# Four narrow q·k rows as one f32 product each on TensorE, where they were two f16 halves

## The chip, the cores and the metric

The kernel runs on one core of a Trainium2 chip. A NeuronCore has a matrix engine (TensorE, in the profile PE, its weight loads apart as PEld), three engines for elementwise work (VectorE or DVE, ScalarE or ACT, GpSimd or POOL) and a queue for DMAs (SyncE or SP). They run side by side and wait for each other through semaphores; each takes its own instructions strictly in the order in which they are written. The metric is the device time of one execution in microseconds, the median of several.

## The reference, cut to what matters

One layer of a model with x of 4 x 1024 x 256: half a gated feed-forward part, an attention part with a delta rule, and again half a feed-forward part, each behind a LayerNorm.

```python
x = x + 0.5 * ffn(layernorm(x))
x = x + attn(layernorm(x))
x = x + 0.5 * ffn(layernorm(x))

# ffn: ternary weights with a scale for each output
h = silu(lin(x, w1)) * lin(x, w2)
h = gelu(lin(h, h1)); h = gelu(lin(h, h2)); return lin(h, w3)

# attn: 16 heads of 16, one step for each of the 1024 tokens
retrieval = einsum('bhij,bhj->bhi', S, k_t)
S = S + einsum('bhi,bhj->bhij', beta_t * (v_t - retrieval), k_t)
o_t = einsum('bhij,bhj->bhi', S, q_t)
```

## The kernel before

**Tiling.** The tokens are cut into 8 slabs of 128 tokens for each of the 4 sequences. The feed-forward layers run over a slab at a time (512 columns; at the two ends over half a slab, 256 columns), with fp8 weights and the activations split into two f16 halves, high and low, so every product is two matmuls: L1066 for the first layer, L1083 for the others. The attention runs over 16 parts, each a half slab, in chunks of 16 tokens. What the step of the reference does one token at a time is done by chunks: the products of all pairs of tokens inside a chunk (k·k and q·k) are formed first, then a triangular solve, and the state S is brought in once a chunk.

**The rows.** A row t of k·k or q·k holds the products of token t of every chunk with the tokens before it (for q·k with itself too). Row t of q·k has 32 times (t + 1) columns, so the rows qk 0 to qk 3 have 32, 64, 96 and 128 columns, and row 15 has 512. The 128 partitions are 8 heads of 16; the sum over the 16 elements of a head is a matmul with a constant matrix of ones and zeros (`head_ones`, for k·k `head_minus`). A row goes through these steps:

- GpSimd multiplies k or q by k, elementwise, into a buffer of `pairs` (L594), f32.
- A row that is in `SPLIT` is then cut into halves: ScalarE casts it to f16 (`pairs_hi`, L728), GpSimd subtracts and casts the rest (`pairs_lo`, L602), and TensorE multiplies `head_ones16` with the one and the other into the same bank (L1118, L1119).
- A row that is not in `SPLIT` goes to TensorE as it is, one f32 matmul (L1121). The profile shows an f32 matmul as two records of TensorE and two weight loads.
- VectorE takes the sum from the bank (L885 and L887 for q·k, L867 to L871 for k·k).

Before the change `SPLIT` holds the k·k rows 6 to 15 and all 16 rows of q·k. The k·k rows 1 to 5 (32 to 160 columns) go as f32. There are 16 parts, so each row occurs 16 times; only k·k row 0 does not exist.

**What sets the order.** The order on every engine is written out ahead of time. The feed-forward work is a stream of slots; a frame of attention is 88 ticks laid over this stream, and at each tick the attention's work is put between the slots. In the frame of a part, its q·k rows stand at the ticks `E_QK` of the frame behind (1, 4, 6, 7 for rows 0 to 3, then 12, 14, 16 ...), its k·k rows at `E_KK` of the frame ahead (54 to 87, the f32 rows last). A planner gives the ticks of the steps ahead of the matmul: the product of a split row is made 9 ticks ahead (`PAIR_LEAD["half"]`), its high half is cast 4 and its low half 3 ticks ahead; the product of a whole row is made 4 ticks ahead (`PAIR_LEAD["whole"]`). The times move later where a buffer is not free by the plan: there are 6 buffers of `pairs` and 5 of each half. A buffer of `pairs` is free after the low half is made if its row was split, and after the matmul if it was whole:

```python
if before in SPLIT:
    pool.wait_ge(pairs_ready, q - PAIR_BUFFERS + 1)
else:
    pool.wait_ge(att_filled, U[before] + 1)
```

GpSimd makes in the same queue the low halves of the feed-forward activations (`hid_lo`, L565), for which TensorE waits too, and ScalarE the functions and the high halves in front of them (L680, L656).

Of the kernel before, what the change touches and what calls it, by code (L numbers as in the profile page):

```python
# [178 lines left out]
    READ.update({use: 1 + i for i, use in enumerate(u for u in USES if READER[u[0]] == _reader)})  # L179
DOTS = [use for use in USES if use[0] in ("kk", "qk")]  # L180
DOT = {use: q for q, use in enumerate(DOTS)}
SPLIT_FROM = {"kk": 6, "qk": 0}
SPLIT = {use: q for q, use in enumerate(u for u in DOTS if u[2] >= SPLIT_FROM[u[0]])}
SPLITS = list(SPLIT)

# [1032 lines left out]
```

## Time and profile before

| | us |
|---|---|
| median of 3 runs | 1817.11 |
| lowest, highest | 1815.38, 1817.98 |
| the profiled execution | 1814.47 |
| its span, first to last instruction | 1812.8 |
| TensorE busy in it | 1729.3 |
| VectorE, ScalarE, GpSimd busy | 1242.2, 1055.7, 1208.6 |

The rows of the trace stand in numbered groups further down. A busy time of TensorE counts a matmul up to its modelled end, so that matmuls overlap in it; what a matmul costs the engine is read from the start of the one behind it. "Idle before" is the time in which an engine stood still ahead of an instruction, with what ended it.

### The profile page before, as it was taken

The numbers are of one execution on the slowest core, as the hardware profiler recorded it, in microseconds if no ns is written. First come the engines' busy times: TensorE is split into PE (matmuls) and PEld (weight loads), VectorE is DVE, ScalarE is ACT, GpSimd is POOL, SyncE is SP. The second block draws the span as 40 slices with busy tenths as digits, with TensorE's granted clock in tenths as the row PEclk, the third lists the DMA queues.
The fourth block names the chain that finished last, engine by engine and source line by source line (L and its number), as shares of the span: only waits on it lengthen the run. The fifth ranks groups of instructions, "written<-read, shape, count | busy, mean of one in ns | idle before, by whom it ended". The sixth has DMA issues, their size and how long they took to land.

```text
span 1812.8 us, 29738 instructions
## 1 busy us (share of the span) xinstructions
PE 1729.3 (95%) x10030; PEld 1068.9 (59%) x10030; DVE 1242.2 (69%) x2890; ACT 1055.7 (58%) x2115; POOL 1208.6 (67%) x1501
## 2 busy tenths in 40 slices
PE   6989989999999999999999999999999999999999
PEld 5855555555555555555555555578655555555588
DVE  5255776777776877868767687777776768777331
ACT  4656555474656565656556474656656555655454
POOL 4463876767676767777676667667776767675653
PEclk9999999999999999999999999999999999999999
DMA  7100000000000000000000000000000000000000
GB/s 289 44 1 1 1 1 1 1 1 2 0 1 1 24 1 24 1 1 1 1 2 1 1 24 1 1 25 1 1 1 1 1 1 13 1 1 12 1 13 13
DMA packets 5270, 23.16 MB, mean 13 GB/s; under 512 B 640, under 2 KB 1664, under 8 KB 3584
## 3 DMA queue, kind: packets, MB, share of 16 engines
q1 hardware_dynamic: 5120, 21.26, 3.2%
q8 instruction: 82, 1.34, 0.3%
q14 instruction: 68, 0.56, 0.1%
HBM read 17.06 MB, written 4.19 MB: 12 GB/s over the span
## 4 chain that ended last, share of the span: by engine, by line
PE 65%; DVE 10%; issue 8%; POOL 8%; ACT 7%; POOLq 0%; ACTq 0%; DVEq 0%
PE ffn_bank L1083 40%; PE ffn_bank L1066 5%; PE att_bank L1131 5%; PE att_bank L1103 4%; POOL hid_lo L565 3%; PE state_bank L1139 2%; PE att_bank L1118 2%; POOL pairs_lo L602 2%; PE ln_bank L1024 2%; PE att_bank L1119 2%; POOL pairs L594 2%; ACT hid L680 2%; DVE hid L821 1%; ACT L680 1%; DVE terms L920 1%
## 5 line engine op out<-in xcount | busy, mean ns | idle before, releaser
L1083 PE MATMUL ffn_bank<-hid_hi,w_sb 128*128 128x512 f16 (+1 forms) x2736 | 905.9, 346 | 7.8 <-ACT gate L667 4.6
L1083 PE MATMUL ffn_bank<-hid_lo,w_sb 128*128 128x512 f16 (+1 forms) x2736 | 905.8, 346 | 0.0
L565 POOL TENSOR_TENSOR hid_lo<-hid,hid_hi 128x512 f16<-128x512 f32 (+1 forms) x456 | 462.7, 1030 | 296.2 <-ACT hid_hi L656 295.9
L594 POOL TENSOR_TENSOR pairs<-KQ 128x32 f32<-128x32 f32 (+15 forms) x496 | 325.7, 667 | 123.8 <-DVE KQ L848 104.8
L1083 PEld LDWEIGHTS ffn_bank<-hid_hi,w_sb 128*128 128x128 fp8e4 x2736 | 275.9, 101 | 206.5 <-issue 11.3
L1083 PEld LDWEIGHTS ffn_bank<-hid_lo,w_sb 128*128 128x128 fp8e4 x2736 | 268.6, 98 | 205.7 <-issue 12.4
L602 POOL TENSOR_TENSOR pairs_lo<-pairs,pairs_hi 128x448 f16<-128x448 f32 (+15 forms) x416 | 313.0, 757 | 74.0 <-ACT pairs_hi L728 73.7
L728 ACT CAST pairs_hi<-pairs 128x448 f16<-128x448 f32 (+15 forms) x416 | 174.8, 438 | 158.9 <-POOL pairs L594 157.6
L656 ACT CAST hid_hi<-hid 128x512 f16<-128x512 f32 (+1 forms) x456 | 234.9, 552 | 30.7 <-DVE hid L821 30.0
L680 ACT ACTIVATE hid<-ffn_bank,par_sb 128x512 f32<-128x512 f32 (+1 forms) x304 | 171.7, 616 | 123.5 <-PE ffn_bank L1083 122.8
L1066 PE MATMUL ffn_bank<-xn_hi,w_sb 128*128 128x512 f16 (+1 forms) x532 | 177.6, 348 | 9.1 <-DVE hid L821 6.6
L1066 PE MATMUL ffn_bank<-xn_lo,w_sb 128*128 128x512 f16 (+1 forms) x532 | 177.3, 348 | 0.0
L922 DVE TENSOR_REDUCE state_bank<-terms 128x16 f32<-128x32 f32 (+7 forms) x512 | 159.4, 311 | 17.6
L885 DVE TENSOR_TENSOR qk_u<-att_bank,U_sb 128x32 f32<-128x32 f32 (+15 forms) x256 | 110.4, 431 | 88.4 <-PE att_bank L1119 88.1
L920 DVE TENSOR_TENSOR terms<-NK,state_bank 128x32 f32<-128x32 f32 (+7 forms) x512 | 152.6, 298 | 10.2
L1103 PE MATMUL att_bank<-xn,wqkvb_sb 128*128 128x256 f32 x512 | 123.4, 384 | 7.0 <-ACT xn L646 6.9
L1131 PEld LDWEIGHTS att_bank<-KQ,state_bd 128*128 128x128 f32 x1024 | 123.3, 192 | 9.7 <-issue 3.7
L667 ACT ACTIVATE gate<-ffn_bank,par_sb 128x512 f32<-128x512 f32 (+1 forms) x152 | 94.1, 619 | 55.0 <-PE ffn_bank L1066 26.9
L871 DVE TENSOR_TENSOR NK<-att_bank,beta 128x448 f32<-128x448 f32 (+14 forms) x240 | 98.7, 419 | 34.7 <-PE att_bank L1119 28.1
L1131 PE MATMUL att_bank<-KQ,state_bd 128*128 128x32 f32 x1024 | 120.2, 271 | 0.1
L887 DVE TENSOR_REDUCE O_in<-qk_u 128x32 f32<-128x32 f32 (+15 forms) x256 | 112.5, 439 | 8.8
L799 DVE RECIPROCAL roots<-roots 128x128 f32<-128x128 f32 (+2 forms) x86 | 84.3, 1014 | 48.6 <-ACT roots L641 48.6
(92 smaller groups left out, 2134.9 us busy)
## 6 DMA issues: line engine op xcount, KB each, us to landing
NK<-in_w SPq DMA_DIRECT2D x11, 1024.0 KB, 5.9
X<-in_x SPq DMA_DIRECT2D x7, 512.0 KB, 3.6
out<-X SPq DMA_DIRECT2D x7, 512.0 KB, 2.6
wqkvb_sb<-in_wqkvb SPq DMA_DIRECT2D x1, 1024.0 KB, 8.6
X<-in_x SPq DMA_DIRECT2D x2, 256.0 KB, 6.5
out<-X SPq DMA_DIRECT2D x2, 256.0 KB, 2.1
wout_sb<-in_wout SPq DMA_DIRECT2D x1, 256.0 KB, 9.3
par_sb<-in_par SPq DMA_DIRECT2D x1, 24.0 KB, 2.5
```

Of the source, the lines that this page charges most:

```text
L565: pool.tensor_tensor(hid_lo[layer % 2][:, m, call.cols], hid[:, u % HID_BUFFERS, call.cols], hid_hi[layer % 2][:, m, call.cols], ALU.subtr ...
L594: pool.tensor_tensor(packed(pair(pairs, q, dot), n), later, earlier, ALU.mult).then_inc(pairs_made if dot in SPLIT else pairs_ready, 1)
L602: pool.tensor_tensor(pair(pairs_lo, i, dot), pair(pairs, DOT[dot], dot), pair(pairs_hi, i, dot), ALU.subtract).then_inc(pairs_ready, 1)
L656: act.copy(hid_hi[layer % 2][:, m, call.cols], hid[:, u % HID_BUFFERS, call.cols]).then_inc(hid_hi_ready, 1)
L680: act.activation(hid[:, (u + i) % HID_BUFFERS, cols], ffn_ps(call, j), ACT.Gelu, scale=p(("h1_s", "h2_s")[layer - 1], m)).then_inc(ffn_rea ...
L728: act.copy(pair(pairs_hi, i, dot), pair(pairs, DOT[dot], dot)).then_inc(pairs_hi_ready, 1)
L920: nc.vector.tensor_tensor(part, rows, known.to_broadcast([P, 2, GB, n]), ALU.mult).then_inc(solve_step, 1)
L922: nc.vector.tensor_reduce(u_view[:, :, 2 * m:n].rearrange("p g v -> p v g"), part, AX.X, ALU.add).then_inc(solve_step, 1)
L1066: mm = nc.tensor.matmul(ffn_ps(call, k), weight(name, kk, m), v[:, kk, cols], start=kk == 0 and part == 0, stop=kk == KT_IN - 1 and part == 1)
L1083: mm = nc.tensor.matmul(ffn_ps(call, j), weight(name, kk, 2 * pair + i), v[:, kk, cols], start=kk == 0 and part == 0, stop=kk == KT_FF - 1 ...
L1103: mm = nc.tensor.matmul(ps[:, g * HALF:(g + 1) * HALF], wqkvb_sb[:, k, j * P:(j + 1) * P], xn[:, k, cols], start=k == 0, stop=k == KT_IN - 1)
L1131: mm = nc.tensor.matmul(ps[:, g * 2 * C:(g + 1) * 2 * C], state_bd[:, g, :], KQ[:, :, at:at + C], start=True, stop=True)
```

## The change

The planner's table `SPLIT_FROM` says from which row on a row is split. For q·k it goes from 0 to 4. Everything else follows from it: `SPLIT` loses 64 of its 416 entries, the planner sets new ticks, and the branches in the four engines' code take the other way for rows 0 to 3 of q·k.

```diff
-SPLIT_FROM = {"kk": 6, "qk": 0}
+SPLIT_FROM = {"kk": 6, "qk": 4}
```

For each of the 64 rows one cast of ScalarE, one subtraction of GpSimd and two f16 matmuls go away and one f32 matmul with `head_ones` comes. The product of the row is made 4 ticks ahead of its matmul instead of 9. Over the whole program TensorE's list is 64 instructions shorter.

On TensorE, around row 3 of q·k in the third part (parts are counted from 1; the names are the bank written and what is read, then the columns), before:

```order
L1083 MATMUL ffn_bank<-hid_hi,w_sb 128x512
L1083 MATMUL ffn_bank<-hid_lo,w_sb 128x512
L1118 MATMUL att_bank<-pairs_hi,head_ones 128x128
L1119 MATMUL att_bank<-pairs_lo,head_ones 128x128
L1083 MATMUL ffn_bank<-hid_hi,w_sb 128x512
L1083 MATMUL ffn_bank<-hid_lo,w_sb 128x512
```

The same place now:

```order
L1083 MATMUL ffn_bank<-hid_hi,w_sb 128x512
L1083 MATMUL ffn_bank<-hid_lo,w_sb 128x512
L1121 MATMUL att_bank<-pairs,head_ones 128x128
L1083 MATMUL ffn_bank<-hid_hi,w_sb 128x512
L1083 MATMUL ffn_bank<-hid_lo,w_sb 128x512
```

The place between the feed-forward matmuls is the same, and only the pair of f16 matmuls has become one in f32.

On GpSimd, from the last k·k row of the fourth part (128x32) over the rows of q·k of the third part, before:

```order
L594 TENSOR_TENSOR pairs<-KQ 128x32 x2
L594 TENSOR_TENSOR pairs<-KQ 128x64
L594 TENSOR_TENSOR pairs<-KQ 128x96
L602 TENSOR_TENSOR pairs_lo<-pairs,pairs_hi 128x32
L594 TENSOR_TENSOR pairs<-KQ 128x128
L565 TENSOR_TENSOR hid_lo<-hid,hid_hi 128x512 x2
L602 TENSOR_TENSOR pairs_lo<-pairs,pairs_hi 128x64
L602 TENSOR_TENSOR pairs_lo<-pairs,pairs_hi 128x96
L594 TENSOR_TENSOR pairs<-KQ 128x160
L602 TENSOR_TENSOR pairs_lo<-pairs,pairs_hi 128x128
L594 TENSOR_TENSOR pairs<-KQ 128x192
L594 TENSOR_TENSOR pairs<-KQ 128x224
```

And now:

```order
L594 TENSOR_TENSOR pairs<-KQ 128x32 x2
L565 TENSOR_TENSOR hid_lo<-hid,hid_hi 128x512 x2
L594 TENSOR_TENSOR pairs<-KQ 128x64
L594 TENSOR_TENSOR pairs<-KQ 128x96
L594 TENSOR_TENSOR pairs<-KQ 128x128
L594 TENSOR_TENSOR pairs<-KQ 128x160
L594 TENSOR_TENSOR pairs<-KQ 128x192
L594 TENSOR_TENSOR pairs<-KQ 128x224
```

The four low halves are gone, and the products of rows 1 to 3 stand behind the two `hid_lo` where they stood ahead of them. In six of the 16 parts (1, 3, 7, 8, 9 and 15) row 1 has come behind two `hid_lo` like this; in seven it is another of the narrow rows that has one or two more ahead of it, and in three (2, 6 and 10) none. The product of 224 columns now takes the buffer of row 0, and so waits for that row's matmul instead of its low half.

## Rows read from the trace of the kernel before

**Rows 1.** The page: busy time, share, instructions; then the last chain by engine.
```profile
PE 1729.3 (95%) x10030; PEld 1068.9 (59%) x10030; DVE 1242.2 (69%) x2890; ACT 1055.7 (58%) x2115; POOL 1208.6 (67%) x1501
...
PE 65%; DVE 10%; issue 8%; POOL 8%; ACT 7%; POOLq 0%; ACTq 0%; DVEq 0%
```

**Rows 2.** Timeline of PE, third part: start, duration, line, tiles, shape, count.
```profile
426.55 0.18 PE L1118 MATMUL att_bank<-pairs_hi,head_ones 128*128 128x32 f16 x1
...
426.60 0.38 PE L1083 MATMUL ffn_bank<-hid_hi,w_sb 128*128 128x512 f16 x1
...
428.32 0.19 PE L1118 MATMUL att_bank<-pairs_hi,head_ones 128*128 128x64 f16 x1
...
428.38 0.38 PE L1083 MATMUL ffn_bank<-hid_hi,w_sb 128*128 128x512 f16 x1
...
430.19 0.22 PE L1118 MATMUL att_bank<-pairs_hi,head_ones 128*128 128x128 f16 x1
...
430.31 0.38 PE L1083 MATMUL ffn_bank<-hid_hi,w_sb 128*128 128x512 f16 x1
```

**Rows 3.** Timeline of PE, k·k rows in f32, each with the matmul behind it.
```profile
420.89 0.33 PE L1121 MATMUL att_bank<-pairs,head_minus 128*128 128x64 f32 x2
421.06 0.38 PE L1083 MATMUL ffn_bank<-hid_hi,w_sb 128*128 128x512 f16 x1
...
422.98 0.30 PE L1121 MATMUL att_bank<-pairs,head_minus 128*128 128x32 f32 x2
423.12 0.38 PE L1083 MATMUL ffn_bank<-hid_hi,w_sb 128*128 128x512 f16 x1
...
806.22 0.39 PE L1121 MATMUL att_bank<-pairs,head_minus 128*128 128x128 f32 x2
806.44 0.38 PE L1083 MATMUL ffn_bank<-hid_hi,w_sb 128*128 128x512 f16 x1
```

**Rows 4.** The chain in four windows over qk 0 to 3 (parts 3, 16, 6, 8).
```profile
by line: PE ffn_bank L1083 94.3%; PE att_bank L1118 3.7%; PE att_bank L1119 2.5%
...
by line: PE ffn_bank L1083 99.4%; PE att_bank L1119 3.1%; PE att_bank L1118 2.8%
...
by line: DVE terms L920 22.6%; DVE hid L821 20.3%; issue 15.0%; DVE state_bank L922 12.9%; DVE X L829 12.7%; DVE qk_u L885 5.8%; PE ffn_bank L1066 3.5%; DVE state_bank L906 2.8%; DVE att_bank L902 2.8%; DVE O_in L887 1.3%; PE att_bank L1131
...
919.97 1.07 POOL hid_lo L565
...
921.08 0.44 POOL pairs_lo L602
...
921.56 0.23 PE att_bank L1118
```

**Rows 5.** Groups by form, POOL and ACT: the steps that go away (or half of them).
```profile
L602 POOL TENSOR_TENSOR pairs_lo<-pairs,pairs_hi 128x128 f16<-128x128 f32 x16 | 6.8, 427 | 22.7 <-ACT pairs_hi L728 22.7
...
L602 POOL TENSOR_TENSOR pairs_lo<-pairs,pairs_hi 128x32 f16<-128x32 f32 x16 | 3.9, 247 | 0.0
...
L728 ACT CAST pairs_hi<-pairs 128x128 f16<-128x128 f32 x16 | 4.8, 302 | 0.3 <-POOL pairs L594 0.3
...
L728 ACT CAST pairs_hi<-pairs 128x32 f16<-128x32 f32 x16 | 3.5, 217 | 35.1 <-POOL pairs L594 35.0
```

**Rows 6.** Groups of PE: q·k and k·k split rows, busy and mean, idle before.
```profile
L1118 PE MATMUL att_bank<-pairs_hi,head_ones 128*128 128x32 f16 (+15 forms) x256 | 70.9, 280 | 4.4 <-POOL pairs_lo L602 4.2
...
L1118 PE MATMUL att_bank<-pairs_hi,head_minus 128*128 128x448 f16 (+9 forms) x160 | 49.4, 308 | 22.5 <-POOL pairs_lo L602 16.3 <-ACT O L720 4.0 <-DVE NK L871 1.1
```

**Rows 7.** Line L1121: idle time before its loads and matmuls until this, times.
```profile
  POOL pairs L594: 12.2, 17
```

**Rows 8.** Timelines of POOL and PE: the last `hid_lo` ahead of row 1, and row 1.
```profile
811.82 2.27 POOL L565 TENSOR_TENSOR hid_lo<-hid,hid_hi 128x512 f16<-128x512 f32 x2 [0.75 <-ACT hid_hi L656]
...
817.64 0.19 PE L1118 MATMUL att_bank<-pairs_hi,head_ones 128*128 128x64 f16 x1
```

**Rows 9.** Who waited for whom: GpSimd for the keys.
```profile
POOL pairs L594 <- DVE KQ L848: 104.8, 13, 12.7
```

## The prediction

> **What bounds the kernel now.** I read the page first, then the chain of work that ended last, window by window, then TensorE's own timeline, because what a small matmul costs there can't be read from its busy time. TensorE is busy 1729.3 of 1812.8 us, and the chain lies on it for 65% [rows 1]. The other four shares of the chain (VectorE, GpSimd, ScalarE, "issue") are 7 to 10% each. So 83.5 us of idle time are all that any relief of the other engines could give, and each nanosecond added to TensorE's own work counts wherever the chain runs through that place on TensorE.
>
> **Cost on TensorE, step by step.** The cost of a matmul here is the time from its start to the start of the next feed-forward matmul. Two f16 halves of 32 columns take 426.60 - 426.55 = 0.05 us, of 64 columns 0.06, of 128 columns 0.12 [rows 2]; the row of 96 columns lies between, 0.09. The trace of before has no f32 matmul with `head_ones`, but the same operation with `head_minus`, of the same columns and between the same neighbours: 32 columns 0.14 us, 64 columns 0.17, 128 columns 0.22 [rows 3], and 96 columns between, 0.19. The differences are 0.09, 0.11, 0.10 and 0.10, together 0.40 us a part and 16 x 0.40 = 6.4 us over the program. I take these values as they are: only the constant matrix differs.
>
> The Trainium skill, "FP8 and Floating Point Precision", section "TensorE Precision Notes", says that true f32 is four passes through the array; two f16 halves are two. By that rule alone the four rows would cost twice their pairs, 0.32 us a part more, so 5.1 us in all instead of 6.4. The rows agree at 128 columns (0.22 against 0.12) and not at 32 (0.14 against 0.05), so the rule names the lesser price for the narrowest row.
>
> **What of it lies on the path.** I went over the chain in the 16 windows from row 0 to row 3 of q·k. In 11 parts (2 to 5, 7, 9, 11, 12, 14 to 16) it is TensorE's from end to end, rows 0 to 3 included, as in parts 3 and 16: L1083 with L1118 and L1119 make up the whole window [rows 4] (its first two rows). (In part 5 the feed-forward share is mostly L1066.) In parts 8 and 10 the chain leaves TensorE after row 0 for ScalarE and `hid_lo`, and returns with the low half of row 3 [rows 4] (its last three rows); rows 0 and 3 count there, 0.09 + 0.10, rows 1 and 2 don't. In parts 6 and 13 the chain is VectorE's, the solve and the feed-forward products [rows 4] (its third row), and in part 1 it is GpSimd's. There a longer TensorE meets a wait that stands anyway. The sum: 11 x 0.40 + 2 x 0.19 = 4.8 us. The bounds of this step are 4.8 minus whatever the other engines give back, and 6.4 if parts 1, 6, 8, 10 and 13 count in full. A path that is longer by 4.8 us and from which nothing is taken away can't end earlier, which is why I hold the forecast rather near this value.
>
> **What goes away elsewhere.** GpSimd loses 64 subtractions of 247 to 427 ns [rows 5], with the two middle widths between some 16 x 1.35 = 21 us, and ScalarE 64 casts of 217 to 302 ns, some 16.6 us. Neither sets the end: they are busy 67% and 58% [rows 1]. Two waits go with them. GpSimd stands 22.7 us ahead of the low half of row 3 until ScalarE has cast it, and ScalarE 35.1 us ahead of the cast of row 0 until GpSimd has made the product [rows 5], with the GELUs of the feed-forward queued behind it. What is late next in both cases is the feed-forward work, which waits for TensorE's banks and so can't run ahead of it. What TensorE could gain is bounded by its own waits. Ahead of all q·k rows they are 4.4 us, 4.2 of them for low halves [rows 6]; those rows follow the narrow ones at once, so this is where a lighter GpSimd would show. The 16.3 us for low halves of k·k rows [rows 6] come later in a frame, and between the two GpSimd stands idle for the keys, 104.8 us in 13 waits [rows 9]: whatever it was behind by, it has caught up there, whether or not it made the narrow low halves. I take zero of the 16.3, and a part of the 4.2 as the lower side of my range.
>
> **What is moved.** The product of a narrow row now comes 4 ticks ahead of its matmul, behind `hid_lo` work that stood behind it; in six parts row 1 has two `hid_lo` more ahead of it. TensorE would wait for it with its whole queue of feed-forward matmuls behind. In the part where this is tightest, part 7, the two `hid_lo` end at 811.82 + 2.27 = 814.09 and the matmul of row 1 starts at 817.64 [rows 8]: 3.55 us for one product, where an elementwise step of 128 columns takes 0.43 [rows 5]. So I cost it at nothing. The same holds for the new wait of GpSimd for the matmuls of rows 0 to 3 (products of 224 to 320 columns): by the plan they come 6 or 7 ticks after these matmuls. Without that cover the price is that of the f32 k·k rows: 12.2 us in 17 waits over 80 rows [rows 7], or 12.2 x 64 / 80 = 9.8 us for 64 rows.
>
> **The sum against its own time.** The profiled execution took 1814.5 us, 1.7 more than its span; with 4.8 it is 1819.3. The median of the three runs is 1817.1, 2.6 above the profiled one, so the forecast is 1817.1 + 4.8 = 1821.9 us.
>
> **The rivals.**
>
> *The other engines give back most of it (same).* The narrow rows cost TensorE 4.8 us, and all waits for low halves ahead of q·k rows go, 4.2 us: 0.6 us in all, 1817.7. For it: GpSimd and ScalarE lose about 1.3 and 1.0 us in each part just ahead of these waits. Against it: those waits are few, the widest rows have them too, and a wait that goes is worth its full length only if nothing else was about to end beside it. It decides from a return of 1.2 us on, which brings the rest under the bound of 3.6.
>
> *GpSimd was the real limit (faster).* Its lighter queue takes away the waits for low halves also in the k·k rows. Half of the 4.2 + 16.3 us is 10.2, against the 6.4 of all narrow rows: -3.8 us, 1813.3. It decides from 10.0 us of returned waits on. For it: L1118 waits for GpSimd longer than for anything else, and GpSimd's list is shorter by 64. Against it: the idle time for the keys stands between.
>
> *The products come too late (slower by more).* In the six parts row 1 waits like an f32 k·k row that waits, 12.2 / 17 = 0.72 us each, 4.3 us in all: 9.1 with the 4.8, 1826.2. It decides where `hid_lo` in front of row 1 ends less than about 0.4 us ahead of the matmul; 3.55 us is the smallest distance now. For it: the plan gives these rows the same 4 ticks that the f32 k·k rows have, and some of those wait.
>
> That the change doesn't do what it says can be left out: the pairs are seen to be replaced in the written order.
>
> **How the numbers follow.** A measurement of this kernel can tell about 0.2%, 3.6 us, from no change. The forecast gets 0.61, the first rival 0.25, faster 0.06, late products 0.08. Within the forecast's own spread of about 2.5 to 6.4 us, nine tenths lie over 3.6 us. So slower is 0.55 + 0.08 = 0.63, same 0.06 + 0.25 = 0.31, faster 0.06. The range takes in the first rival down to 0.2 us below its price, and above the 6.4 us another 1.1 for a short wait in some parts: 1817.5 to 1824.6. It leaves out the faster case, most of the late products and a little of the first rival.
>
> **What would show it.** In the profile of the changed kernel L1121 with `head_ones` has 128 records, and the next feed-forward matmul starts 0.14, 0.17, 0.19 and 0.22 us behind these rows; TensorE's idle time ahead of them is near zero; the idle time ahead of the rest of the q·k rows is at most 4.4 us; GpSimd is about 21 us less busy and ScalarE about 17. The forecast is wrong if `head_ones` in f32 costs other than `head_minus`, if L1121 waits for GpSimd more than the 12.2 us of before by over 2 us, or if the waits ahead of k·k rows shrink by several us.

## The result, and the profile after

| | us |
|---|---|
| before, median of 20 runs (lowest, highest) | 1815.8 (1813.4, 1818.2) |
| changed, median of 20 runs | 1820.7 (1818.1, 1824.1) |
| ratio | 1.0025, 95% interval 1.0019 to 1.0032 |
| span of the profiled executions | 1812.8 before, 1816.4 changed |

The change made the kernel slower, by 4.9 us between the medians, 3.4 to 5.8 us by the interval of the ratio (4.5 by the ratio itself). 4.8 us were forecast, from a median of 1817.1 on three runs; on twenty it is 1815.8, and the forecast on that base would have been 1820.6.

The page of the changed kernel, busy times and the chain by engine, answers to [rows 1]:

```profile
PE 1734.9 (96%) x10030; PEld 1079.8 (59%) x10030; DVE 1243.1 (68%) x2890; ACT 1044.3 (57%) x2051; POOL 1192.1 (66%) x1437
...
PE 68%; DVE 9%; issue 8%; POOL 7%; ACT 7%; DMA 0%; POOLq 0%; ACTq 0%; DVEq 0%; SPq 0%
```

GpSimd lost 16.5 us of busy time and ScalarE 11.4, TensorE gained 5.6, and the chain has moved on to TensorE from 65% to 68%. TensorE still has 10030 records, since one f32 matmul is two records, as two f16 matmuls are.

Its timeline at the four rows of the third part (start, duration, line, tiles, shape, count), each row with the matmul behind it, answers to [rows 2, 3]:

```profile
425.22 0.30 PE L1121 MATMUL att_bank<-pairs,head_ones 128*128 128x32 f32 x2
425.36 0.38 PE L1083 MATMUL ffn_bank<-hid_hi,w_sb 128*128 128x512 f16 x1
...
427.08 0.33 PE L1121 MATMUL att_bank<-pairs,head_ones 128*128 128x64 f32 x2
427.25 0.38 PE L1083 MATMUL ffn_bank<-hid_hi,w_sb 128*128 128x512 f16 x1
...
428.11 0.36 PE L1121 MATMUL att_bank<-pairs,head_ones 128*128 128x96 f32 x2
428.31 0.38 PE L1083 MATMUL ffn_bank<-hid_hi,w_sb 128*128 128x512 f16 x1
...
429.17 0.38 PE L1121 MATMUL att_bank<-pairs,head_ones 128*128 128x128 f32 x2
429.39 0.38 PE L1083 MATMUL ffn_bank<-hid_hi,w_sb 128*128 128x512 f16 x1
```

0.14, 0.17, 0.20 and 0.22 us: the prices of the `head_minus` rows. The groups of TensorE by line (busy, mean ns, idle before with what ended it) show what it waited for, and answer to [rows 6]:

```profile
L1121 PE MATMUL att_bank<-pairs,head_ones 128*128 128x32 f32 (+3 forms) x128 | 21.1, 256 | 0.0
...
L1118 PE MATMUL att_bank<-pairs_hi,head_ones 128*128 128x160 f16 (+2 forms) x192 | 58.8, 306 | 4.1 <-POOL pairs_lo L602 4.0
...
L1118 PE MATMUL att_bank<-pairs_hi,head_minus 128*128 128x448 f16 (+9 forms) x160 | 49.7, 311 | 21.1 <-POOL pairs_lo L602 14.9 <-ACT O L720 4.1 <-DVE NK L871 1.1
```

TensorE never waited ahead of an f32 row of q·k (0.0), and the waits ahead of the split rows are nearly what they were: 4.4 has become 4.1, 22.5 has become 21.1. The 1.4 us between the last two lie at 108 to 112 us, ahead of the first row that was changed (223.8 us): TensorE had run at the lower clock just before (0.51 granted from 102.5 to 106 us, full clock in the kernel before) and came later itself. From row 0 of the first part on, the waits ahead of the k·k rows are the same one by one.

The time can be followed part by part. This table has the start of row 0 of q·k in every part, in us, from the timelines of the two kernels; "step" is how much the distance grew up to the next row (for part 16 up to the end of the span).

| part | before | changed | distance | step | chain of before at rows 0 to 3 |
|---|---|---|---|---|---|
| 1 | 224.4 | 223.8 | -0.6 | -1.2 | GpSimd |
| 2 | 327.0 | 325.2 | -1.8 | +0.5 | TensorE |
| 3 | 426.5 | 425.2 | -1.3 | +0.4 | TensorE |
| 4 | 518.0 | 517.1 | -0.9 | +0.5 | TensorE |
| 5 | 618.4 | 618.0 | -0.4 | +0.4 | TensorE |
| 6 | 716.8 | 716.8 | 0.0 | 0.0 | VectorE |
| 7 | 815.9 | 815.9 | 0.0 | +0.5 | TensorE |
| 8 | 916.8 | 917.3 | +0.5 | +0.2 | TensorE at rows 0 and 3 |
| 9 | 1019.5 | 1020.2 | +0.7 | +0.5 | TensorE |
| 10 | 1116.9 | 1118.1 | +1.2 | +0.2 | TensorE at rows 0 and 3 |
| 11 | 1219.4 | 1220.8 | +1.4 | +0.5 | TensorE |
| 12 | 1322.4 | 1324.3 | +1.9 | +0.4 | TensorE |
| 13 | 1419.8 | 1422.1 | +2.3 | 0.0 | VectorE |
| 14 | 1520.7 | 1523.0 | +2.3 | +0.4 | TensorE |
| 15 | 1616.8 | 1619.6 | +2.7 | +0.5 | TensorE |
| 16 | 1698.8 | 1702.0 | +3.2 | +0.4 | TensorE |

From part 2 on the steps have the sizes that the chain of before gave: 0.4 to 0.5 us where it lay on TensorE, 0.2 where it lay there at two of the four rows, nothing at all in parts 6 and 13. They add up to 5.4 us.

In parts 8 and 10 the size is right, but it comes about in another way than forecast. Part 8 of before, and then of the changed kernel, where rows 2 and 3 are shown as one line of four records:

```profile
921.26 0.21 PE L1118 MATMUL att_bank<-pairs_hi,head_ones 128*128 128x96 f16 x1
...
921.56 0.23 PE L1118 MATMUL att_bank<-pairs_hi,head_ones 128*128 128x128 f16 x1
```

```profile
921.92 0.61 PE L1121 MATMUL att_bank<-pairs,head_ones 128*128 128x96 f32 x4
922.37 0.38 PE L1083 MATMUL ffn_bank<-hid_hi,w_sb 128*128 128x512 f16 x1
```

Before, row 3 starts 0.30 us after row 2, which elsewhere takes 0.09: it stood 0.21 us for its low half. In the changed kernel rows 2 and 3 together take 0.45 us, so there is no wait left between them. All four rows are dearer here too, by 0.44 us, and the wait of 0.21 has gone; what is left is the 0.2.

The profiled pair is only 3.6 us apart because of what happens up to the end of part 1, and most of that is not the work of the change. The view by windows (length, then busy time and instructions of PE, PEld, DVE, ACT, POOL, the granted clock, DMA) of before at 262 to 270 us, in part 1:

```profile
262.00:264.00 2.00, 0.00 (x0) 0.00 (x0) 1.97 (x5) 0.69 (x2) 0.00 (x0) 1.00 0.00 0
264.00:268.00 4.00, 3.55 (x9) 2.76 (x10) 3.29 (x4) 1.43 (x3) 1.72 (x2) 0.57 0.02 4
268.00:270.00 2.00, 2.00 (x11) 0.97 (x9) 0.64 (x1) 1.92 (x5) 2.00 (x3) 1.00 0.00 0
```

and the same of the changed kernel:

```profile
264.00:268.00 4.00, 3.93 (x18) 2.57 (x19) 3.51 (x5) 2.92 (x8) 2.10 (x2) 1.00 0.00 0
```

In the profiled execution of before the granted clock is 0.57 there, so mostly the lower of the two levels, 1.2 GHz, after TensorE had stood idle (0.00 busy from 262 to 264). The f32 projections ran at half speed, 9 matmuls in 4 us instead of 18. The changed kernel was idle there too and kept the full clock. The distance between the two goes from -0.4 to -1.9 us over these projections, 1.5 us. Without this the step of part 1 is +0.3 us and not -1.2, so the rows seem to count there too.

### The profile page after: what moved, and what is told of

Its sections match the earlier page's. It is cut to its first block, busy times and chain, and to the rows that moved or that the text cites. A ratio compares the mean times of both kernels' runs of the same rounds, so it can differ in the third digit from the quotient of the medians.

```text
span 1816.4 us, 29482 instructions
## 1 busy us (share of the span) xinstructions
PE 1734.9 (96%) x10030; PEld 1079.8 (59%) x10030; DVE 1243.1 (68%) x2890; ACT 1044.3 (57%) x2051; POOL 1192.1 (66%) x1437
## 4 chain that ended last, share of the span: by engine, by line
PE 68%; DVE 9%; issue 8%; POOL 7%; ACT 7%; DMA 0%; POOLq 0%; ACTq 0%; DVEq 0%; SPq 0%
PE ffn_bank L1083 40%; PE ffn_bank L1066 6%; PE att_bank L1131 5%; PE att_bank L1103 4%; POOL hid_lo L565 3%; PE state_bank L1139 2%; PE ln_bank L1024 2%; PE att_bank L1118 2%; POOL pairs_lo L602 2%; PE att_bank L1119 2%; POOL pairs L594 2%; PE att_bank L1121 1%; ACT hid L680 1%; DVE hid L821 1%; ACT L680 1%
## 5 line engine op out<-in xcount | busy, mean ns | idle before, releaser
L602 POOL TENSOR_TENSOR pairs_lo<-pairs,pairs_hi 128x448 f16<-128x448 f32 (+10 forms) x352 | 292.9, 836 | 52.9 <-ACT pairs_hi L728 52.7
L656 ACT CAST hid_hi<-hid 128x512 f16<-128x512 f32 (+1 forms) x456 | 234.9, 552 | 30.4 <-DVE hid L821 29.9
L728 ACT CAST pairs_hi<-pairs 128x448 f16<-128x448 f32 (+10 forms) x352 | 159.0, 471 | 117.2 <-POOL pairs L594 116.8
L720 ACT COPY O<-att_bank 128x128 f32<-128x128 f32 x64 | 17.0, 266 | 187.9 <-DVE state_bank L906 187.8
```

What stands on the lines that cost most here:

```text
L602: pool.tensor_tensor(pair(pairs_lo, i, dot), pair(pairs, DOT[dot], dot), pair(pairs_hi, i, dot), ALU.subtract).then_inc(pairs_ready, 1)
L656: act.copy(hid_hi[layer % 2][:, m, call.cols], hid[:, u % HID_BUFFERS, call.cols]).then_inc(hid_hi_ready, 1)
L728: act.copy(pair(pairs_hi, i, dot), pair(pairs, DOT[dot], dot)).then_inc(pairs_hi_ready, 1)
```

## The experiments

All were timed in turns with the kernel before; its median in these comparisons was 1815.4 for the first four, 1815.35 for the next two and 1815.7 for the last.

### The relief alone

```diff
-SPLIT_FROM = {"kk": 6, "qk": 0}
+SPLIT_FROM = {"kk": 6, "qk": 4}
...
                 ps = att_use(*dot)
+                if dot[0] == "qk" and dot[2] < 4:
+                    nc.tensor.matmul(ps[:, 0:n], head_ones16[:, :], head_ones16[:, 0:n], start=True, stop=False)
+                    nc.tensor.matmul(ps[:, 0:n], head_ones16[:, :], head_ones16[:, 0:n], start=False, stop=True).then_inc(att_filled, 1)
+                    return
```

> The changed kernel in everything (orders, ticks, no casts and no low halves for the rows qk 0 to 3), but TensorE makes two f16 matmuls of the row's width again, on the constant head_ones16 in place of the row's products; so the values of rows 0 to 3 of q.k are left out. Theory (the price is TensorE's own time, the relief of the others is worth next to nothing): as fast as the kernel before, -0.7 to +0.5 us. Rival (the relief gives back part of a dearer matmul cost): clearly faster than before, by 2 us or more.

Measured: 1814.1 us, ratio 0.9995 (0.9987 to 1.0004), that is -0.9 us, from -2.4 to +0.7. The lighter GpSimd and ScalarE, the new order and the later products together are worth nothing that can be told from zero. In the trace the steps of the table above are 0.0 from part 2 to part 7 and again from part 11 on; between parts 8 and 11, where low halves of the narrow rows had been on the chain, they sum to -0.4 us: 0.23 at the four rows of part 8 and 0.23 at those of part 10, where the wait of 0.21 us stood. GpSimd is 17.0 us less busy than before (1191.6), and TensorE waits for the low halves of the k·k rows as long as ever, 16.4 us where it was 16.3 (L1122 is L1118 of before, shifted by the edit):

```profile
L1122 PE MATMUL att_bank<-pairs_hi,head_minus 128*128 128x448 f16 (+9 forms) x160 | 49.4, 309 | 22.5 <-POOL pairs_lo L602 16.4 <-ACT O L720 4.1 <-DVE NK L871 1.1
```

### The cost alone

```diff
                 ps = att_use(*dot)
+                if dot[0] == "qk" and dot[2] < 4:
+                    nc.tensor.matmul(ps[:, 0:n], head_ones[:, :], head_ones[:, 0:n], start=True, stop=True).then_inc(att_filled, 1)
+                    return
```

> The kernel before in everything (casts, low halves, orders), but for the rows qk 0 to 3 TensorE makes one f32 matmul of the row's width, on the constant head_ones, in place of the two f16 ones; the values of these rows are left out. Theory: the whole loss is here, +4.4 to +6 us (4.8 where the chain runs over TensorE, up to 6.4). Rival (products made later, or behind hid_lo, carry part of the loss): under +3 us here.

Measured: 1821.1 us, ratio 1.0031 (1.0019 to 1.0043): +5.6 us, from +3.4 to +7.8. The whole loss is here, with every order, cast and low half left as it was. The groups of TensorE of this run (the edit shifts the lines by three, so L1121 is the high half of a split row here, and L1117 the new f32 matmul):

```profile
L1121 PE MATMUL att_bank<-pairs_hi,head_ones 128*128 128x160 f16 (+2 forms) x192 | 58.8, 306 | 4.1 <-POOL pairs_lo L602 4.0
...
L1117 PE MATMUL att_bank<-head_ones 128*128 128x32 f32 (+3 forms) x128 | 21.1, 256 | 0.0
```

The f32 rows have the busy time of the changed kernel, 21.1 us, and nothing waits more. -0.9 and +5.6 add up to 4.7, where both together gave 4.9. In the trace the steps at the four rows are those of the changed kernel in all 16 parts, also the 0.2 in parts 8 and 10: the low half of row 3 is still made there, but the dearer rows 0 to 2 take up the time in which TensorE had waited for it. Part 1 comes to +0.5 us (0.87 to 1.38 apart at row 0 of parts 1 and 2), and here both executions ran at the lower clock at the same places.

### Eight rows instead of four

```diff
-SPLIT_FROM = {"kk": 6, "qk": 0}
+SPLIT_FROM = {"kk": 6, "qk": 8}
```

> The rows qk 0 to 7 as f32 instead of 0 to 3. Theory: an f32 row of 160 columns costs 0.27 us against 0.14, and by the same step (0.05 us more for 32 columns in f32, 0.03 in two halves) rows 4 to 7 cost 0.13, 0.16, 0.18 and 0.21 us more, 0.68 a part, 10.9 us in all; the chain of before lies on TensorE at these rows in 15 of 16 parts, so about 10 us behind the 4.8: +13 to +17 us. Rival (GpSimd's relief counts): GpSimd loses 59 us here and ScalarE 39; with 17.3 us more on TensorE the loss would stay under +10 us.

Measured: 1826.5 us, ratio 1.0072 (1.0059 to 1.0086): +13.1 us, from +10.7 to +15.6 (+11.1 between the medians). The two widest of the new f32 rows in its timeline:

```profile
441.21 0.54 PE L1121 MATMUL att_bank<-pairs,head_ones 128*128 128x224 f32 x2
441.59 0.38 PE L1083 MATMUL ffn_bank<-hid_hi,w_sb 128*128 128x512 f16 x1
...
443.32 0.59 PE L1121 MATMUL att_bank<-pairs,head_ones 128*128 128x256 f32 x2
443.75 0.38 PE L1083 MATMUL ffn_bank<-hid_hi,w_sb 128*128 128x512 f16 x1
```

0.38 and 0.43 us, as expected (0.37 and 0.43 by the step from row to row). By the time the loss is at the lower end of the theory: of 17.3 us more on TensorE it shows 11 to 13. The trace says otherwise. The profiled execution is the slowest of the six, with a span 19.0 us over that of before. From row 0 of part 1 to the end it loses 17.8 us, 2.0 of them to one VectorE instruction (L808 at 1267 us) that took 3.21 us where it took 0.82 before. The other 15.8 are nine tenths of the 17.3, and lie in the range of the theory. In 13 of the 16 parts rows 4 to 7 add 0.7 us, which is their full price. So the share that the chain of before gave for these rows was right.

What the times have too little is probably the clock. Four executions took 1826.1 to 1826.6 us, at a mean granted clock of 0.997; the two others took 1832.5 and 1833.5 us, at 0.995 and 0.993; the executions of the kernel before in the same comparison have 0.994 to 0.996, mostly 0.995. An estimate from that: 0.002 more of the clock over 1826 us is 3.7 us, about what is missing. Why this kernel dropped less often to the lower clock in four of six executions no run shows. It was hardly GpSimd's relief: TensorE's waits ahead of the k·k rows are 1.8 us less than before (20.7 against the 22.5 of [rows 6]), but all of that lies at 108 to 112 us, ahead of the first changed row and again behind a stretch at the lower clock; the waits ahead of the split q·k rows are 0.9 us less (3.5 against 4.4).

### The other way: the five f32 rows of k·k split

```diff
-SPLIT_FROM = {"kk": 6, "qk": 0}
+SPLIT_FROM = {"kk": 1, "qk": 0}
```

> The other way: the rows kk 1 to 5 are split too, nothing is left in f32 among the rows; q.k as before. Theory (TensorE's time is what counts): these rows cost 0.09, 0.11, 0.11, 0.11 and 0.13 us less each, and the chain of before lies on them in 15, 14, 13, 9 and 14 parts: 7 us faster than before, -5 to -8. Rival (GpSimd is near its limit at the end of a frame, where these rows come a tick or two apart): 29 us more on GpSimd make its low halves late, and TensorE waits for them: from -3 to several us slower.

Measured: 1822.7 us, ratio 1.0038 (1.0025 to 1.0051): +6.9 us. My theory was wrong here and the rival right. TensorE is 4.9 us less busy than before (1724.4), and the kernel is slower. Its timeline of TensorE near row 4 in frame 3:

```profile
415.96 0.38 PE L1083 MATMUL ffn_bank<-hid_lo,w_sb 128*128 128x512 f16 x1
418.95 0.29 PE L1118 MATMUL att_bank<-pairs_hi,head_minus 128*128 128x128 f16 x1 [2.61 <-POOL pairs_lo L602]
...
419.14 0.63 PE L1083 MATMUL ffn_bank<-hid_hi,w_sb 128*128 128x512 f16 x1
419.56 0.63 PE L1083 MATMUL ffn_bank<-hid_lo,w_sb 128*128 128x512 f16 x1
```

and of GpSimd:

```profile
416.24 2.27 POOL L565 TENSOR_TENSOR hid_lo<-hid,hid_hi 128x512 f16<-128x512 f32 x2
418.46 0.43 POOL L602 TENSOR_TENSOR pairs_lo<-pairs,pairs_hi 128x128 f16<-128x128 f32 x1
```

The kernel before has at this place:

```profile
415.64 0.46 POOL L594 TENSOR_TENSOR pairs<-KQ 128x128 f32<-128x128 f32 x1
416.05 2.28 POOL L565 TENSOR_TENSOR hid_lo<-hid,hid_hi 128x512 f16<-128x512 f32 x2
```

As a whole row, row 4 needs only its product, which stands ahead of two `hid_lo`. Split, its last step is the low half, and that stands behind them: 2.27 us later. TensorE waits 2.61 us, and then pays a second time: the feed-forward matmuls behind it start 0.42 us apart instead of 0.21, since the clock has fallen to 1.2 GHz. The windows of this run:

```profile
415.00:419.00 4.00, 1.39 (x8) 0.45 (x6) 2.60 (x8) 2.06 (x9) 4.00 (x6) 0.92 0.00 0
419.00:423.00 4.00, 4.00 (x19) 2.10 (x19) 1.08 (x4) 1.49 (x4) 2.85 (x10) 0.65 0.00 0
```

Over the whole run the idle time of TensorE that ended with a k·k low half is 32.4 us (16.3 before), 13.1 of it ahead of row 4 alone. TensorE fell to the lower clock in the midst of or behind three such waits in this run: 2.61 us up to 418.95, 3.47 us up to 1014.73, and 1.71 us up to 1519.34 ahead of row 5.

### Only rows 1 to 3 of k·k split

```diff
-SPLIT = {use: q for q, use in enumerate(u for u in DOTS if u[2] >= SPLIT_FROM[u[0]])}
+SPLIT = {use: q for q, use in enumerate(u for u in DOTS if u[2] >= SPLIT_FROM[u[0]] or u[2] < 4)}
```

> Of the k.k rows only 1 to 3 are split besides 6 to 15; rows 4 and 5 stay in f32, q.k as before. With kk 1 to 5 split the run was slower, and its trace put 13.1 us of waiting for low halves ahead of row 4 alone, 0.0 us ahead of rows 2 and 3. Theory (TensorE's own time counts where the row's products are early enough; the loss lay at row 4): rows 1 to 3 cost 4.6 us less on TensorE by the pitches of that trace, nearly all of it on the chain: -2.5 to -5 us. Rival (anything more on GpSimd at the end of a frame delays row 4 or the rows of q.k behind it): from -1 us to slower, with the wait ahead of L1121 grown by several us.

Measured: 1811.95 us, ratio 0.9978 (0.9969 to 0.9987): -4.0 us, from -5.6 to -2.4. This version beats both kernels, and it is the change of this document turned round, on other rows. Its groups of TensorE:

```profile
L1118 PE MATMUL att_bank<-pairs_hi,head_minus 128*128 128x448 f16 (+12 forms) x208 | 58.2, 282 | 23.8 <-POOL pairs_lo L602 16.3 <-ACT O L720 4.0 <-DVE NK L871 2.5
...
L1121 PE MATMUL att_bank<-pairs,head_minus 128*128 128x128 f32 (+1 forms) x64 | 14.4, 307 | 6.1 <-POOL pairs L594 3.9 <-DVE NK L871 2.1
```

The waits for GpSimd are the 16.3 and 3.9 us of before. TensorE saves 4.6 us on the three rows by their prices. In the trace 3.0 us of it arrive between row 0 of part 1 and the end (the distance to the kernel before goes from +1.8 to -1.2 us); the time, -5.6 to -2.4, fits both.

### Half the weight columns

```diff
                 ps = att_use(*dot)
+                if dot[0] == "qk" and dot[2] < 4:
+                    nc.tensor.matmul(ps[0:64, 0:n], head_ones[:, 0:64], pair(pairs, DOT[dot], dot), start=True, stop=True).then_inc(att_filled, 1)
+                    return
```

(on the changed kernel)

> The changed kernel, but the f32 matmuls of the rows qk 0 to 3 load 64 of the 128 columns of head_ones and write 64 partitions; the other half of these sums is left out. It asks what sets the 0.14 us of a row of 32 columns in f32. If it is the loading of the weights (two loads of 190 ns each in the trace), the row of 32 columns falls to 0.10 us or less and the loss against before shrinks to about +3 us. If it is the passes over the columns or a fixed cost of an f32 matmul, the four rows keep 0.14, 0.17, 0.19 and 0.22 us and the loss stays near +5 us.

Measured: 1830.7 us, ratio 1.0083 (1.0067 to 1.0098): +15.1 us. Neither expectation holds. The timeline of TensorE at row 0 of the third part, and of its weight loads:

```profile
427.72 0.38 PE L1083 MATMUL ffn_bank<-hid_lo,w_sb 128*128 128x512 f16 x1
428.03 0.30 PE L1117 MATMUL att_bank<-pairs,head_ones 128*64 128x32 f32 x2
428.26 0.39 PE L1083 MATMUL ffn_bank<-hid_hi,w_sb 128*128 128x512 f16 x1
```

```profile
427.50 0.10 PEld L1083 LDWEIGHTS ffn_bank<-hid_lo,w_sb 128*128 128x128 fp8e4 x1
428.03 0.19 PEld L1117 LDWEIGHTS att_bank<-pairs,head_ones 128*64 128x64 f32 x2 [0.42 <-issue]
428.26 0.10 PEld L1083 LDWEIGHTS ffn_bank<-hid_hi,w_sb 128*128 128x128 fp8e4 x1
```

A load of 64 columns is short (two in 0.19 us), but it doesn't begin while the matmul ahead runs: load and matmul both start at 428.03, 0.31 us after the feed-forward matmul that else gives way after 0.21, and the next full load starts only with its matmul, at 428.26. The row took 0.23 us instead of 0.14, and with the 0.10 ahead of it costs 0.19 more. The experiment changed two things at once, the size of the load and when it begins, and so leaves open what sets the 0.14.

### All k·k rows but row 4 split

```diff
-SPLIT = {use: q for q, use in enumerate(u for u in DOTS if u[2] >= SPLIT_FROM[u[0]])}
+SPLIT = {use: q for q, use in enumerate(u for u in DOTS if u[2] >= SPLIT_FROM[u[0]] or u[2] in (1, 2, 3, 5))}
```

> As e5, and row kk 5 is split too, so that row 4 alone is left in f32. Theory (the loss with all five rows split came from the low half of row 4 itself, which has to be cast and subtracted after its product): row 5 costs 0.13 us less in each of 14 parts, 1.9 us on top of e5: -4.5 to -6.5 us against the kernel before. Rival (any more work for GpSimd near rows 4 and 5 is late, whichever row it is for): the wait ahead of rows 4 and 5 grows by 5 us or more, and the run is no faster than e5.

Measured: 1821.1 us, ratio 1.0026 (1.0015 to 1.0038): +4.7 us. The rival again. The group of TensorE by form for row 5, and GpSimd's timeline at the place:

```profile
L1118 PE MATMUL att_bank<-pairs_hi,head_minus 128*128 128x160 f16 x16 | 3.9, 241 | 9.8 <-POOL pairs_lo L602 9.2 <-DVE NK L871 0.6
```

```profile
418.05 1.44 POOL L594 TENSOR_TENSOR pairs<-KQ 128x128 f32<-128x128 f32 x4
419.44 2.27 POOL L565 TENSOR_TENSOR hid_lo<-hid,hid_hi 128x512 f16<-128x512 f32 x2
...
421.87 0.49 POOL L602 TENSOR_TENSOR pairs_lo<-pairs,pairs_hi 128x160 f16<-128x160 f32 x1
```

Row 4 waits no more than before, but row 5 has taken over its part: 9.8 us of waiting, where it had 3.1 as an f32 row. So the loss doesn't belong to row 4. In both runs it belongs to the row whose last step on GpSimd falls behind the pair of `hid_lo` while its matmul has little room. The waits alone are less than the 8.7 us between this run and the one with rows 1 to 3: ahead of all k·k rows they are 35.4 us where they were 29.9, and row 5 itself has become cheaper. Two of them, of 2.50 us each (up to 219.56 and 1516.48), ran into stretches at the lower clock, and the mean granted clock is 0.992 to 0.995 here and 0.994 to 0.997 there.

## Why the prediction was right

**The price of a row.** Taken from `head_minus` rows of the same widths, 0.40 us a part. The changed kernel shows 0.14, 0.17, 0.20 and 0.22 us, so 0.41 more than the pairs. In seven parts row 3 follows row 2 without a feed-forward matmul between, and takes 0.25 instead of 0.22; this I had not seen. It is 7 x 0.03 = 0.2 us. All rows together cost 6.8 us, not 6.4.

**What of it is on the path.** This step did the work, and it held in the 11 parts of TensorE and in parts 6 and 13: the steps are 0.4 to 0.5 and 0.0 where the chain of before said so. "The cost alone" shows that it is TensorE's time and nothing else. It failed in three parts. In 8 and 10 the forecast let rows 0 and 3 count, 0.19 us, because a wait that stands hides the other two. But the wait was for the low half of row 3, which the change takes away; all four rows count, 0.44, and 0.21 comes back. That both ways give 0.2 is luck. So "nothing is taken away" from the path was not true either. In part 1 nothing was to count, and about 0.3 to 0.5 us did. In the traces 5.7 to 5.8 us of the 6.8 arrive, more than eight tenths where the forecast had three quarters.

**The four passes.** By the rule of the Trainium skill ("FP8 and Floating Point Precision", "TensorE Precision Notes": four passes for true f32) the four rows would have cost 0.32 us a part more. They cost 0.41 more. From 128 columns on the rows are at the ratio of the rule: 0.22 us against 0.12 for 128 columns, and in "Eight rows instead of four" 0.43 against 0.22 for 256 columns. So the rule holds for the wide rows, and the narrow ones have a floor on top.

**What goes away elsewhere.** I took it at nothing, with 4.2 us as its bound. "The relief alone" gives 0.9 us with an interval that holds zero, and 0.4 us of it can be placed in the trace. The reason given for the rest, that the feed-forward work waits for TensorE's banks and can't run ahead, shows in ScalarE's wait ahead of its GELUs, which grew by 35 us from before to changed:

```profile
L680 ACT ACTIVATE hid<-ffn_bank,par_sb 128x512 f32<-128x512 f32 (+1 forms) x304 | 171.7, 616 | 123.5 <-PE ffn_bank L1083 122.8
...
L680 ACT ACTIVATE hid<-ffn_bank,par_sb 128x512 f32<-128x512 f32 (+1 forms) x304 | 172.0, 617 | 158.3 <-PE ffn_bank L1083 157.6
```

The engines' busy time fell by less than forecast, 16.5 us for 21 and 11.4 for 17, although the low halves and casts themselves shrank by 20.1 and 15.8 (in the groups of the two pages). Nothing in the sum hung on it.

**What is moved.** Right for TensorE: 0.0 us of waiting ahead of the f32 rows. The count of parts was short, since row 1 came behind one or two more `hid_lo` in ten parts and not in six, but it had room in all of them. One sentence of it was not: that GpSimd's new wait costs nothing because the products of 224 to 320 columns come 6 or 7 ticks after the matmuls of rows 0 to 3. The group of GpSimd in the changed kernel:

```profile
L594 POOL TENSOR_TENSOR pairs<-KQ 128x224 f32<-128x224 f32 x32 | 19.0, 592 | 15.6 <-PE att_bank L1121 15.5
```

GpSimd, with the low halves gone, runs ahead of its plan and stands 15.5 us there. It cost TensorE nothing all the same: "The relief alone" has the same wait, 14.8 us, and is no slower than before. A distance in planned ticks tells nothing of an engine that isn't held to them.

**The rivals.** "The other engines give back most of it" would need 1.2 us returned. 0.9 came by the middle of the interval, whose end of 2.4 doesn't rule it out; the trace does, with 0.4. "GpSimd was the real limit" fell with the same run: 17 us less on GpSimd gave TensorE none of its waits for k·k rows back. "The products come too late" didn't happen on the q·k rows, where 3.5 us of room were read. But the mechanism is real a few ticks earlier in the frame, as the two k·k experiments show, and there it costs more than TensorE's saving.

**The size.** 4.8 forecast and 4.9 measured is closer than the parts of the sum: parts 2 to 16 show 5.4 in the trace, with part 1 5.7, "The cost alone" gave 5.6, and the interval of the measurement is 2.4 us wide. That the two agree to 0.1 us is luck.

## What to carry to other kernels

- Cost a small matmul by the distance to the start of the next one, and find an operation of the same shape in the trace before believing a rate. Then look, place by place, whether the chain passes over it there; with TensorE at 95% the share was three quarters by the time and over eight tenths by the traces, not all.
- Where the chain leaves the busy engine for a wait, ask whether the change takes that wait away. If it does, the whole cost counts there, and the wait comes back.
- Work taken from an engine at 67% with a plan of its own was worth nothing except where a wait for it stood at that place. Work added to it can cost more than its length, if it puts the last step of something narrow behind a long pair of instructions.
- So the choice between f32 and two f16 halves is made row by row: halves where the low half has room in GpSimd's queue (k·k rows 1 to 3, -4.0 us), f32 where it has none (rows 4 and 5).

## What the runs showed of the hardware

- The time of an f32 matmul with a 128x128 weight goes with its columns as 0.14, 0.17, 0.20, 0.22 us for 32 to 128 columns, and 0.27, 0.38, 0.43 for 160, 224 and 256 (`437.19` to `437.46` for the first of these in the run with eight rows). Below 128 a step of 32 columns adds about 0.027 us, above it 0.053. The floor lies behind the second of the two records, not between them. Timelines of PE over windows that leave out the first record (425.50:425.53 and 429.50:429.55) show the second one of the rows of 32 and 128 columns in the changed kernel, whose first records start at 425.22 and 429.17 and whose next matmuls at 425.36 and 429.39:

```profile
425.24 0.28 PE L1121 MATMUL att_bank<-pairs,head_ones 128*128 128x32 f32 x1
...
429.28 0.28 PE L1121 MATMUL att_bank<-pairs,head_ones 128*128 128x128 f32 x1
```

At 32 columns the second record starts 0.02 us after the first and the next matmul 0.12 after that; at 128 columns it is 0.11 and 0.11. What holds the next matmul back for this 0.11 to 0.12 us no run shows.
- A weight load of 64 columns was not drawn ahead of the running matmul, as loads of 128 columns are; in the row of 32 columns 0.10 us were lost ahead of the row and 0.09 in it, and the load behind was held up too.
- One wait of TensorE of 2.61 us was followed by a stretch in which feed-forward matmuls of 512 columns started 0.42 us apart instead of 0.21, at a granted clock of 0.65 over 4 us. A wait on the busiest engine can thus be paid twice. It is not paid twice each time: the wait at 262 to 264 us was followed by half clock in the kernel before and by full clock in the changed one, and one of 3.1 us at 102 us the other way round. The stretch at 264 us cost about 1.5 us, so it is worth looking for before two traces are compared.
